# Moving eight batches of edges from the passage between two halves of a graph layer into its expert groups

## The reference, cut to what matters

```python
xn = _layernorm(x)                                        # x: 6250 nodes x 256, 100000 edges sorted by dst
all_msg = einsum('nf,rfo->rno', xn, weight)               # 16 relations
msg = all_msg[rel_type, src] * norm * sigmoid(gate)       # one row of 256 per edge
agg = relu(segment_sum(msg, dst))
k, v = inst_norm(k), inst_norm(v)                         # of xn @ w_qkv, 8 heads of 64
mix = (q @ (k.T @ v) / n) @ w_out + b_out                 # k.T @ v is a sum over all nodes
x = x + agg + mix
h = gelu(tokens @ w1[e] + b1[e]); y = h @ w2[e] + b2[e]   # 8 experts, weights of the top 2
out = x + layernorm(x) + sum over e of combine[:, e] * y
```

## Time and profile before

| | before |
| --- | --- |
| median of 3 runs | 1873.97 us (1873.87 to 1875.1) |
| profiled execution, own time | 1872.99 us |
| its span in the trace | 1871.2 us |
| PE busy | 1789.5 us, 96% of the span |
| DVE busy | 1174.2 us, 63% |
| ACT busy | 772.5 us, 41% |
| POOL busy | 775.2 us, 41% |
| mean granted clock of PE | 0.987 of full speed |

### The profile page before, as it was taken

How to read it: one execution, slowest core, us unless ns; L and a number is a source line. 1 busy time by engine, 2 the same in 40 slices (tenths; PEclk the granted TensorE clock), 3 DMA queues, 4 the chain that set the end, 5 groups by cost and what they waited for, 6 DMA issues and landing times.

```text
span 1871.2 us, 30573 instructions
## 1 busy us (share of the span) xinstructions
PE 1789.5 (96%) x11137; PEld 1601.4 (86%) x11137; DVE 1174.2 (63%) x3496; ACT 772.5 (41%) x1428; POOL 775.2 (41%) x812
## 2 busy tenths in 40 slices
PE   6999999999999799999699999999999999999988
PEld 5887888888888699998689998999899989899988
DVE  6554555544443667666657677677686776767764
ACT  5555666555554433332033334334243342432443
POOL 2000000000000476677776666666566666566600
PEclk9999999999999999999899999999999999999999
DMA  6665777655555664443443343433424333333300
GB/s 224 236 239 211 281 281 281 256 216 219 213 220 206 260 233 143 143 148 116 143 125 113 108 127 89 130 112 109 124 86 135 110 108 110 93 119 114 113 16 17
DMA packets 113914, 296.06 MB, mean 158 GB/s; under 512 B 18120, under 2 KB 73792, under 8 KB 104420
## 3 DMA queue, kind: packets, MB, share of 16 engines
q1 hardware_dynamic: 75236, 189.63, 27.4%
q0 software_dynamic: 38528, 104.46, 18.9%
HBM read 162.70 MB, written 131.32 MB: 157 GB/s over the span
## 4 chain that ended last, share of the span: by engine, by line
PE 87%; DVE 6%; POOL 2%; issue 2%; ACT 1%; DMA 1%; DVEq 0%; SPq 0%; ACTq 0%
PE bank L51 22%; PE bank L53 21%; PE bank L52 21%; PE bank L1343 16%; POOL plain L587 2%; PE bank L1332 2%; PE bank L1408 1%; PE bank L1236 1%; DVE plain L955 1%; PE bank L1448 1%; DVE plain L988 1%; PE bank L1211 1%; PE bank L1389 1%; DVE parts L617 0%; PE bank L1398 0%
## 5 line engine op out<-in xcount | busy, mean ns | idle before, releaser
L587 POOL DMA_INDIRECT plain<-messages,idxT x784 | 764.4, 975 | 984.5 <-issue 825.9
L51 PE MATMUL bank<-parts 128*128 128x512 f32 (+2 forms) x2232 | 812.8, 364 | 30.4 <-DVE plain L988 21.3
L53 PE MATMUL bank<-parts 128*128 128x512 f32 (+2 forms) x2232 | 785.9, 352 | 0.0
L52 PE MATMUL bank<-parts 128*128 128x512 f32 (+2 forms) x2232 | 784.9, 352 | 0.0
L51 PEld LDWEIGHTS bank<-parts 128*128 128x128 f32 x2232 | 426.2, 191 | 83.0 <-issue 33.6
L53 PEld LDWEIGHTS bank<-parts 128*128 128x128 f32 x2232 | 424.4, 190 | 55.0
L52 PEld LDWEIGHTS bank<-parts 128*128 128x128 f32 x2232 | 426.2, 191 | 46.4
L1343 PE MATMUL bank<-plain 128*128 128x128 f32 x3136 | 390.7, 279 | 22.7 <-DMA plain<-messages,idxT 19.0
L1343 PEld LDWEIGHTS bank<-plain 128*128 128x128 f32 x3136 | 376.0, 195 | 29.3 <-DMA plain<-messages,idxT 21.4
L1162 ACT ACTIVATE plain<-bank,small 128x512 f32<-128x512 f32 (+1 forms) x208 | 135.3, 663 | 373.8 <-PE bank L53 370.5
L660 DVE TENSOR_SCALAR plain<-bank,plain 128x256 f32<-128x256 f32 x392 | 171.0, 478 | 163.6 <-PE bank L53 110.0
(11 more groups left out here) (150 smaller groups left out, 984.7 us busy)
## 6 DMA issues: line engine op xcount, KB each, us to landing
messages<-plain SPq DMA_DIRECT2D x49, 2048.0 KB, 6.9
parts<-xnT_scratch SPq DMA_DIRECT2D x20, 1024.0 KB, 5.5
xnT_scratch<-parts SPq DMA_DIRECT2D x98, 128.0 KB, 3.2
plain<-messages,idxT POOLq DMA_INDIRECT x784, 2.8
w_parts<-parts SPq DMA_DIRECT2D x32, 256.0 KB, 2.4
parts<-w_parts SPq DMA_DIRECT2D x4, 2048.0 KB, 20.3
plain<-in_x SPq DMA_DIRECT2D x48, 128.0 KB, 6.9
plain<-in_x SPq DMA_DIRECT2D x10, 512.0 KB, 4.3
```

Of the source, the lines that this page charges most:

```text
L51: e.matmul(out, left(0), right(0), start=start, stop=False)
L52: e.matmul(out, left(0), right(1), start=False, stop=False)
L53: return e.matmul(out, left(1), right(0), start=False, stop=stop)
L587: e.indirect_dma_start(msg[:, b % SLOTS, j, :], None, table_rows, bass.IndirectOffsetOnAxis(idxT[:, j, b:b + 1], 0)).then_inc(s_gather[b % ...
```

## The change

In the passage every step had a batch behind it, 15 in all (43 to 57). Now a batch follows only `fold` 1 and the `ready` steps with an odd number, 7 in all (43 to 49). Thus `first` falls from 58 to 50, and `share()` spreads 146 batches instead of 138 over the same 178 places. The work is the same.

```diff
     more()
     for i in range(3):
         order.append(("fold", i))
-        more()
+        if i == 1:
+            more()
     for i in range(READY):
         ready(0, i)
-        more()
+        if i % 2 == 1:
+            more()
     order += [("up", 0, 0), ("weigh", 0, 0)]
     first = len(closed)
```

## The result

| | before | after |
| --- | --- | --- |
| median | 1874.02 us (6 runs, 1873.31 to 1876.04) | 1888.79 us (6 runs, 1887.70 to 1889.48) |
| ratio after / before | | 1.0076, 95% interval 1.0063 to 1.0089 |
| profiled execution | 1872.99 us | 1888.21 us |
| its span | 1871.2 us | 1886.3 us |
| PE busy | 1789.5 us | 1796.3 us |

The change makes the kernel slower by 14.8 us, 0.8%. The forecast was 10.3 us slower, 1884.3 us, in a range from 1876 to 1891.

What follows compares the result with a forecast made beforehand. The prediction took the gathers (POOL) to bound the passage and PE's work the expert groups. Its terms, -24.7 + 2.2 + 14.2 + 14.5 + 2.2 + 1.9 = +10.3 us, gave 1884.3 us, range 1876 to 1891.

Steps and rivals of the forecast that it cites:

- step 1: Passage: with fewer gathers the chain of steps is left and the first `up` starts 24.7 us earlier; low clock costs +2.2.
- step 2: Expert groups: eight more batches of 1.78 us each where PE is never without work, +14.2 us.
- step 3: Groups 7 to 10: `enough` asks for batches in long rows, and those beyond four slots wait for POOL, +14.5 us.
- The clock behind the rows: Rows of seven and six: the last batch runs at the low clock after PE's idle time, +2.2 us, between 0 and 5.
- step 4: Groups 0 to 8: in one more group `down` of the seventh expert waits 2.38 us for DVE, not 0.48; +1.9 us.
- rival in which the four slots suffice: Expert groups: long rows cost no more than the one of before; 6.4 us faster, 1867.6 us; chance 0.1.
- even case: Whole kernel: clock holds, small waits balance, rows cost a fifth less; +1.1 us, 1875.1 us; chance 0.14.
- fourth rival: Passage: not shorter, as a step waits for something the gathers hide now; a 5 us delay gives 1889; chance 0.05.
- the clock falls everywhere: Passage and groups: both clock bounds (4 and 5) and the small waits' (4) together; +17.0 us, 1891.0 us; chance 0.13.

Runs made afterwards that it cites:

- three-slot kernel: The change with three slots for gathered batches instead of four (SLOTS = 3): 1913.38 us, ratio 1.0209 to the kernel before.
- the rows alone: The kernel before, passage untouched, with share() following the change's formula from place 112 on: 1895.56 us, ratio 1.0118 to the kernel before.

## Why the prediction was right, and where it was short

**The passage** (step 1: -24.7, and +2.2 for the clock). Both traces reach the passage 0.73 us apart (the last `dots` start at 872.23 and 871.50). Less these, the first `up` moved by 21.1 us and the first `bias` by 20.6, where 22.5 were forecast. The chain was read rightly, nearly to the step: second `turn_norm` forecast at 903.5, seen at 903.25; `route` 905.5 and 905.28. Part of that closeness is luck: the trace with the change runs 0.7 to 0.8 us ahead there, and counted from the first `mix` (885.18 instead of 885.96) `route` came 0.6 us later than forecast. What was short was the clock: one spell from 906 to 920 instead of one that begins at `turn_choice`, so that `route` (+0.84), `turn_choice` (+0.41), batch 49 (+1.7) and the first matmuls of `up` (+0.5) paid, 3.5 us instead of 2.2.

**Eight batches more in the groups** (step 2: +14.2). 8 x 1.79 by the ruler: 14.3. The price was right.

**The rows** (step 3: +14.5). 9.2 + 5.3 + 2.2 - 1.6 = 15.1. The seventh batch of group 8 was forecast 19.8 us behind the first and stood at 19.86, the sixth of group 9 at 14.4 and stood at 14.24; group 10's fifth was 0.6 later than forecast. There were six waits for gathers, as said, and none outside the rows. The three-slot kernel moved group 8's seventh as the same arithmetic demands (25.13 us against 24.9).

**The clock behind the rows** (+2.2). Only group 9's last batch paid (3.65 us, +1.6); in group 8 the slow batch was the one before the last, where POOL sets the pace and nothing is lost. As the prediction carried over the Trainium skill (TensorE: Matmul & The Clock Gate, "HAM oscillation — how this bites in real kernels"), both would have paid, and each short burst in between. The waits in that section's kernel are given as about 3 to 5 us, and those here were 1.56 to 2.97. Of the five late batches of these two rows two ran at the low clock and three, behind waits of 2.50, 1.56 and 1.92 us, did not. The trace agrees with it in kind and not for every wait.

**Small waits** (step 4: +1.9). This is the term that was mis-sized. The waits of PE for DVE grew from 14.6 + 2.1 to 18.9 + 1.4 us, +3.6. In groups 0 to 8, which the prediction counted, it was 1.8, as foreseen. It had left out group 10, where one batch less lies between the sixth and the seventh `down` too (2.22 us instead of 0.69), and a `down` in group 7 behind its new row (0.96); the waits for DVE's answer to `bias` fell by 0.7. And I had given these waits no clock (timeline and window of the change):

```profile
986.92 0.36 PE L51 MATMUL bank<-parts 128*128 128x256 f32 x1 [2.38 <-DVE plain L990]
...
988.00:991.00 3.00, 3.00 (x16) 3.00 (x16) 2.90 (x9) 0.00 (x0) 1.28 (x2) 0.52 0.38 117
```

Behind the 2.38 us in group 0 `down` took 4.50 us instead of 3.10; behind the 2.22 us in group 10 `down` took 3.35 instead of 2.39 and the next batch 2.57 instead of 2.05. Before, one such wait (group 7) had cost 1.5 us in the same way. With the clock they were worth 5.0 us net of before's, against 1.9 in the sum and 4 at its upper bound.

The measured terms in the order of the steps: -20.6 in the passage (3.5 of clock, which leaves -24.1 for the chain); 14.3 + 15.1 + 1.6 + 3.6 + 1.4 = 36.0 of the 36.4 us by which the groups grew. With the 0.7 us ahead of the passage the spans' difference of 15.1 is accounted for but for 0.4. In the prediction's own sums one slip stands: with the clocks and the small waits free its terms add up to +4.0, 1878.0, and not to +3.6; nothing hangs on it. The rival in which the four slots suffice is refuted by the rows above, and with it the even case, which had the rows at 11.6 us and no low clock. The passage became shorter, so the fourth rival did not occur either. That in which the clock falls everywhere came nearest in the time (1891.0), but its mechanism did not occur: it needed 9 us of clock, and 6.5 were paid.

The one wait that the prediction put first, 4.53 us ahead of batch 49, is not POOL's issuing alone. The gathers issued around it took longer to land (DMA view of before, 891 to 896.5 and 940 to 1790 us; the last figure is the median from issue to landing):

```profile
plain<-messages,idxT POOLq DMA_INDIRECT x5, 4.8
...
plain<-messages,idxT POOLq DMA_INDIRECT x550, 2.8
```

The end of the passage does not hang on it, since POOL issued on without a pause, and its last batch started 6.5 us after its own first gather.

What the change says it does, it does: 20.6 us gained in the passage for 14.3 in the groups. The loss is a side effect of a formula that starts 8 lower and of a guard, `enough`, that settles the difference in lumps; with the change's passage and no lumps the kernel takes 15.7 us less than before (1857.90 to 1873.59). Of these the move itself accounts for 6.3; the rest is small waits and low clock that the pacing removed, and the ratios of the kernel before with the same pacing say that part of it can be had without the change.

## What to carry to other kernels

When work is moved from a stretch that a producer bounds into one that has slack on average, look at the guards that force it to be done by a date: in a lump that is longer than the store of finished pieces, each piece beyond the store comes at the producer's pace (here 5.0 us for 1.78 of the consumer's work). Shift the pacing together with the starting point, and check the longest row against the number of slots. And the filler between two steps is worth more than its length where it keeps the consumer from running into the next wait: here a batch at each side of `route` saved 1.9 us for a cost that was due anyway.

## What the runs showed of the hardware that was not expected

A gathered batch (four indirect transfers of 128 rows of 1 KB) comes every 5.0 to 5.1 us where POOL issues without a pause, in the kernel before, the change, the rows alone and the three slots. Most batches that PE waited for started 6.5 to 6.7 us after their first issue, all of the change's and the three-slot kernel's in the rows among them. Some took longer: in the passage of the kernel before, batch 49 started 9.2 us after its first issue (9.0 in the rows alone, which has the same passage) and batches 48 and 55 7.4 and 7.7, and in the rows alone batch 159 took 8.1. SP's transfer of 1 MB for a next group was issued at 893.01, between batch 49's gathers; whether it is the cause was not tested.

A low-clock spell can follow a wait of only 2.4 us in a stretch in which PE is else hardly idle: from 988 to 991 us of the change the granted clock is 0.52, behind the wait at 986.92, and from 940 to 988 it was 1.00 with PE busy for 45.6 of 48 us. The same wait of 2.38 us in group 1 (1067.78) was followed by none, the clock from 1067 to 1071 being 1.00.
